# Spline coefficients inside the last context batch, ternary feed-forwards on seven tiles of 128 rows, a gate function and a scaling on ScalarE, spline units in another place

## The chip, the cores and the metric

The kernel runs on one core of a Trainium2 chip. The metric is device time in microseconds (us) of one execution; lower is better. Traces come from the hardware profiler on one such execution. TensorE multiplies, VectorE and ScalarE compute and drain PSUM, GpSimd (POOL) does small work, SyncE (SP) issues most transfers. TensorE's granted clock has two levels, 1.2 and 2.4 GHz; the profile writes them as 0.50 and 1.00.

## The reference

Four transformer layers, each an attention on x and a context and then a feed-forward, with a layer norm before and a residual after each of the eight parts. x is 8 batches of 112 rows of 512 numbers, the context 8 batches of 375 rows.

```
x = x + L0_xattn(ln(x), context)           # part 0, att0
x = x + L0_ffn(ln(x))                      # part 1, ffn0: ternary weights, sigmoid gate
x = x + L1_xattn(ln(x), context)           # part 2, att1: 16 heads, grouped
x = x + L1_ffn(ln(x))                      # part 3, ffn1: ternary weights, silu gate, Hadamard
x = x + L2_xattn(ln(x), context)           # part 4, att2: linear attention
x = x + L2_ffn(ln(x))                      # part 5: one ternary layer
x = x + L3_xattn(ln(x), context)           # part 6, att3
x = x + L3_ffn(ln(x))                      # part 7, ffn3: weights from spline control points

# L0_ffn; quant rounds each row to 8 bits by its own largest magnitude
h = sigmoid(quant(x) @ ternary(w_gate).T) * (quant(x) @ ternary(w_up).T)     # 2048 wide
y = quant(h) @ ternary(w_down).T
# L1_ffn
h = silu(quant(x) @ ternary(w_gate).T) * (quant(x) @ ternary(w_up).T)
y = quant(fwht(h)) @ ternary(w_down).T     # fwht: Walsh-Hadamard transform over the 2048
# L3_ffn: each dense weight is a cubic interpolation of control points
w[n] = cubic in the distance to the control point below, from four points around it
```

## The kernel before

Every engine runs one program written out by hand; they meet at semaphores. An engine executes in order, so what stands behind a waiting instruction waits too. A `Ring` hands PSUM banks round: names in their order of use, each with a lag in iterations; `wait_free`, `wait_filled` and `wait_drained` wait for a bank's last user, for TensorE's result, and for its reader. `link` makes a VectorE instruction wait for the one before it. SP issues transfers in the order of its own program, and waits in it.

**Context** (to 594 us). `context_part` goes over 8 batches; in each TensorE makes three thirds (k1, v1, k2, v2, v3 and transposes T), then k3, the last T and kv_0, kv_1. VectorE has about 4 us of work in each third and drains kv at the end. In batches 0 to 5 a ternary weight is made behind that; in batch 6 two of three spline matrices (L501 to L505) and `powers_of_q` (L520 to L539); in batch 7 the third matrix and `coefficients`, which works out the polynomials (L552 to L561) and splits them in three bf16 parts (L571, L574). ScalarE then repeats two of the parts (L443, L444), and only after that does TensorE transpose them. SP ends the stage with the stores of batch 7, the last of them behind kv_1's drain.

**Weights** (to 617). `weights_part`: SP loads wq3, wp3 and w2 behind `context["filled"]`, then x and the context of two batches of att0, then issues for each of 16 coefficient groups two stores. TensorE transposes a group; ScalarE copies it to one of 8 buffers (L670), and for groups 8 to 15 first waits until the stores of that buffer have landed. After group 3 it waits for the raw weights (L674). At its end ScalarE and TensorE turn two quantized matrices, and att0 starts.

**ffn0 and ffn1** (826 to 951, 1571 to 1814) are both `ternary_ffn`, over 8 tiles, one per batch, of 112 rows. In an iteration b0 is the newest tile and b1, b2, b3 the ones before it (in ffn0 b3 is b2). VectorE's order is: `quantize_x` of b0 (normalize L233, maximum L1025, small numbers, round L1040 and L1043, the result is xi), statistics of the next; four pieces of b1, each 512 columns of gate times up (L1081 and a maximum L1085 in ffn0; L1074 and L1077 in ffn1); in ffn0 `quantize_h`, whose L1049 to L1053 are five small numbers, L1054 scales 2048 columns and adds a constant that rounds, L1057 takes the constant off and clips; in ffn1 the butterflies of b2 (L1098, L1099), the maximum L1101 and `quantize_h`; then y of b3 is added to x (L244). TensorE's order is: for each of four pieces gate and up products of b1 (g, u) and transposes (of clipped h in ffn0; of h of b2 in ffn1); in ffn1 the products with the Hadamard matrix (w) and the transposes of clipped h of b3; then the transposes of xi of b0 (xiT), then y of b3. The next gates wait for this xiT drained. The five names u0 to u3 and y share three banks, so u1 waits for the y before it to be added. ScalarE does for each gate a tanh (L995), in ffn1 behind a copy of the gate (L994), and drains the transposes. x stays in `X`, batch by batch.

The last feed-forward, ffn3, already works on 7 tiles of 128 rows: SP copies pieces of `X` into tiles (L2136); a tile of 128 rows takes rows of two batches.

**att2** (1812 to 1985): `attention2` works on 8 batches in 11 iterations, and eight spline units are put in each iteration on TensorE, ScalarE and VectorE, numbered 8i to 8i+7. A unit makes part of ffn3's weights: one or four small products, a ScalarE copy, a VectorE predicated copy (L1579). Units share two banks, so TensorE's unit u waits for the copy of unit u-2:

```
spline["pe"](pe, 8 * i + 3)
if b2 is not None:            # products a0, a1
...
spline["pe"](pe, 8 * i + 4)
```

## Time and profile before

| | |
|---|---|
| median of three runs | 2653.1 us (2650.66 to 2653.58) |
| the profiled execution | 2655.79 us, span 2654.0 us, mean granted clock 0.952 |
| TensorE busy | 2320.2 us, 87% of the span |
| VectorE busy | 1250.8 us, 47% |
| ScalarE busy | 776.7 us, 29% |
| chain that ended last | TensorE 72%, VectorE 18%, ScalarE 5% |

The busy shares are means over stages with different limits. The chain is followed back from the last instruction, at each step to what released it. In a row, L12 is line 12 of the kernel, PE TensorE, DVE VectorE, ACT ScalarE, SPq SyncE's queue; "<-" names what ended the idle time. Ends of products are modelled; products that follow one another start closer together than their mean duration.

### The profile page before, as it was taken

The numbers are of one execution on the slowest core, as the hardware profiler recorded it, in microseconds if no ns is written. First come the engines' busy times: TensorE is split into PE (matmuls) and PEld (weight loads), VectorE is DVE, ScalarE is ACT, GpSimd is POOL, SyncE is SP. The second block draws the span as 40 slices with busy tenths as digits, with TensorE's granted clock in tenths as the row PEclk, the third lists the DMA queues.
The fourth block names the chain that finished last, engine by engine and source line by source line (L and its number), as shares of the span: only waits on it lengthen the run. The fifth ranks groups of instructions, "written<-read, shape, count | busy, mean of one in ns | idle before, by whom it ended". The sixth has DMA issues, their size and how long they took to land.

```text
span 2654.0 us, 27949 instructions
## 1 busy us (share of the span) xinstructions
PE 2320.2 (87%) x10524; PEld 1358.8 (51%) x10524; DVE 1250.8 (47%) x2497; ACT 776.7 (29%) x1611; POOL 148.7 (6%) x303
## 2 busy tenths in 40 slices
PE   8999999948887869999999986666877788889999
PEld 3555555536554536666666654443433455534444
DVE  1333333562115945555555558974444566621111
ACT  1322333113011323333333324432332455411111
POOL 0000000000000001110001000000000000000000
PEclk9999999979998989999999998887998899989999
DMA  5454433155113010300000030001000211100000
GB/s 200 157 214 159 154 149 122 67 172 211 47 58 159 1 29 19 120 18 24 20 23 24 15 96 17 1 1 31 14 12 7 71 47 47 48 4 4 8 4 12
DMA packets 48042, 171.68 MB, mean 65 GB/s; under 512 B 4561, under 2 KB 24337, under 8 KB 42110
## 3 DMA queue, kind: packets, MB, share of 16 engines
q1 hardware_dynamic: 46182, 132.14, 14.2%
q0 software_dynamic: 1728, 37.75, 3.7%
q8 instruction: 86, 1.41, 0.2%
q14 instruction: 46, 0.38, 0.0%
HBM read 121.58 MB, written 46.47 MB: 63 GB/s over the span
## 4 chain that ended last, share of the span: by engine, by line
PE 72%; DVE 18%; ACT 5%; issue 3%; DMA 1%; SPq 0%; POOL 0%; DVEq 0%; ACTq 0%; POOLq 0%
PE psum L118 61%; PE psum L111 6%; PE psum L1262 4%; DVE R L1098 1%; DVE small L2058 1%; DVE R L1099 1%; ACT WK L2008 1%; DVE small L1101 1%; DVE WK L233 1%; PE psum L1976 1%; DVE WK L1081 1%; DVE small L1085 1%; DVE R L1579 1%; DVE small L1430 1%; ACT R L670 1%
## 5 line engine op out<-in xcount | busy, mean ns | idle before, releaser
L118 PE MATMUL psum<-R,WK 128*125 128x512 f32 (+6 forms) x4000 | 1451.7, 513 | 106.1 <-DVE X L244 40.9
L118 PEld LDWEIGHTS psum<-R,WK 128*112 128x112 f32 (+3 forms) x4000 | 662.6, 176 | 758.1 <-issue 552.6
L111 PE MATMUL psum<-small,WK 112*125 112x112 f32 (+5 forms) x2252 | 309.8, 267 | 132.2 <-DVE WK L233 34.4
L111 PEld LDWEIGHTS psum<-small,WK 112*125 112x125 f32 (+5 forms) x2252 | 249.8, 154 | 241.6 <-issue 130.4
L118 PE MATMUL psum<-WK,R 128*128 128x112 f32 (+4 forms) x1152 | 260.4, 375 | 14.0 <-DVE R L1579 9.0
L118 PEld LDWEIGHTS psum<-WK,R 128*128 128x128 f32 (+2 forms) x1152 | 162.1, 183 | 85.0 <-issue 18.9
L118 PE MATMUL psum<-WK 125*112 125x128 f32 (+5 forms) x1280 | 198.2, 298 | 1.5 <-DVE WK L847 1.2
L118 PEld LDWEIGHTS psum<-WK 125*112 125x112 f32 (+2 forms) x1280 | 162.7, 177 | 66.6 <-issue 49.8
L1430 DVE TENSOR_REDUCE small<-psum 112x1 f32<-112x487 f32 x128 | 85.0, 664 | 221.4 <-PE psum L118 219.5
L1352 ACT ACTIVATE WK<-psum,small 112x487 f32<-112x487 f32 x128 | 96.9, 757 | 259.5 <-DVE small L1432 258.7
L1262 PE MATMUL psum<-R,WK 128*112 128x512 f32 x256 | 120.4, 593 | 0.6 <-ACT WK L1332 0.6
L2008 ACT ACTIVATE WK<-psum,small 112x375 f32<-112x375 f32 x128 | 72.2, 568 | 112.0 <-DVE small L2059 112.0
L2217 DVE SCALAR_TENSOR_TENSOR WK<-WK 128x512 f32<-128x512 f32 x28 | 19.4, 692 | 159.6 <-PE psum L111 141.9
L118 PE MATMUL psum<-R 125*128 125x128 f32 (+2 forms) x320 | 59.9, 298 | 35.4 <-DVE R L1579 33.9
L2058 DVE TENSOR_REDUCE small<-psum 112x2 f32<-112x750 f32 x64 | 59.8, 935 | 61.6 <-PE psum L118 61.3
L223 POOL TENSOR_SCALAR small<-small 112x1 f32<-112x1 f32 (+1 forms) x63 | 14.2, 225 | 1324.1 <-DVE small L217 1324.1
L1438 DVE COPY WK<-psum 125x336 f32<-125x336 f32 x128 | 64.3, 503 | 3.0 <-PE psum L111 3.0
L2187 ACT COPY WK<-psum 128x512 f32<-128x512 f32 x28 | 16.4, 585 | 164.5 <-PE psum L118 164.5
L118 PEld LDWEIGHTS psum<-R 125*128 125x128 f32 (+1 forms) x320 | 34.4, 155 | 56.4 <-DVE R L1579 45.4
L1567 ACT COPY R<-psum 128x256 f32<-128x256 f32 x96 | 35.2, 374 | 87.4 <-PE psum L118 87.2
L464 DVE TENSOR_TENSOR WK<-WK,small 125x512 f32<-125x512 f32 x24 | 16.6, 692 | 92.3 <-PE psum L111 75.3
L820 ACT COPY WK<-psum 128x448 f32<-128x448 f32 x32 | 17.0, 530 | 145.8 <-PE psum L118 76.5
(208 smaller groups left out, 2088.4 us busy)
## 6 DMA issues: line engine op xcount, KB each, us to landing
R<-in_wf POOLq DMA_DIRECT2D x6, 4096.0 KB, 13.7
d_w<-R POOLq DMA_DIRECT2D x6, 2048.0 KB, 17.9
R<-d_w SPq DMA_DIRECT2D x6, 2048.0 KB, 13.0
WK<-in_ctxT SPq DMA_DIRECT2D x16, 750.0 KB, 5.8
d_v<-WK SPq DMA_DIRECT2D x16, 750.0 KB
R<-in_wq SPq DMA_DIRECT2D x7, 1024.0 KB, 6.9
R<-in_wo SPq DMA_DIRECT2D x6, 1024.0 KB, 16.2
d_k<-X SPq DMA_DIRECT2D x8, 750.0 KB, 3.2
```

The source lines that it names most:

```text
L111: ins = pe.transpose(dst, src, idn[0:k, 0:k])
L118: ins = pe.matmul(dst, lhs, rhs, start=k == 0, stop=k == len(pairs) - 1)
L233: return dve.tensor_scalar(dst, x, mv[0:rows, k % 2, 0:1], rv[0:rows, k % 2, 1:2], ALU.subtract, ALU.mult)
L670: act.copy(coefT[0:84, k % 8].rearrange("p s q -> p (s q)"), bank[k % 4][0:84, :].bitcast(BF16)).then_inc(sem("coefT_ready"), 1)
L1081: dve.scalar_tensor_tensor(piece, th[:, c % 2, :], 1.0, dve_ring.bank[f"u{c}"][0:T, :], ALU.add, ALU.mult).then_inc(dve_ring.sem_drained, 1)
L1262: ins = pe.matmul(y, oT[:, g % 2, h, :], wo[:, 4 * g + h, :], start=4 * g + h == 0, stop=4 * g + h == NH - 1)
L1352: act.activation(prob[:, k % 3, :], act_ring.bank[f"s{j}"][0:T, 0:SK], ACT.Exp, bias=nmax[:, k % 3:k % 3 + 1], scale=rq[:, (NG * b + g) % ...
L1430: link(dve.tensor_reduce(mx[:, k:k + 1], act_ring.bank[f"s{j}"][0:T, 0:SK], AX, ALU.max, negate=True))
L1438: dve.tensor_copy(probT[0:SP, j % 2, 0:NS, :], src[0:SP, 0:NS * T].rearrange("p (i t) -> p i t", i=NS))
L1567: ins = act.copy(home(k, t), pieces_of(u)[0])
L2008: act.activation(prob[:, k, a, :], s_ring.bank[f"s{h}"][0:T, 0:S], ACT.Exp, bias=nmax[:, k, a:a + 1], scale=scale, accum_out=total[b % 2][ ...
L2058: link(dve.tensor_reduce(mx[:, j % 2, :], both[:, :, 0:S], AX, ALU.max, negate=True))
```

## The change

The spline coefficients are taken apart: `coefficients(dve, link, w)` does one matrix, `split_coefficients` the split. Batch 6 makes all three spline matrices; the powers, the coefficients and the split lie between the thirds of batch 7. The loads of the raw weights wait for `raw_free`, which is two results of the last third, in place of the context's last results. Ring semaphores are shared by stages.

Both ternary feed-forwards work on 7 tiles of 128 rows. SP copies pieces of `X` into seven tiles xf (`sync`) and, tile by tile after its add, back (`back`); the attention behind each of them waits for all of these copies on every engine (`x_ready` with n of 2 or 4). In ffn1 the gate is one `Silu` on ScalarE, without the copy and without L1074. The scaling of L1054 is done by ScalarE (`scale`, 2048 columns, `Identity` with a scale and a bias per row); VectorE gives it its number (`scale_of_h`) and clips afterwards (`quantize_h`). On VectorE `quantize_x` stands behind the pieces, in ffn0 behind `scale_of_h` and ahead of the clip; in ffn1 the clip of b3 stands between the pieces and `quantize_x`. TensorE's order in these stages is as before.

In att2 unit 8i+4 stands ahead of a0 and a1 on TensorE and VectorE, and unit 8i+6 ahead of the add on VectorE.

```diff
+            if n in (2, 4):
+                eng.wait_ge(sem(f"{'ffn0' if n == 2 else 'ffn1'}_back"), 16 * sum(len(list(pieces(i))) for i in range(NT)))
+            elif n:
...
+                        if b == NB - 1:
+                            if s == 0:
+                                powers_of_q(dve, link)
+                                coefficients(dve, link, 0)
+                            if s == 1:
+                                coefficients(dve, link, 1)
+                                coefficients(dve, link, 2)
+                            if s == 2:
+                                split_coefficients(dve, link)
...
+                    elif b == 6:
+                        dve.wait_ge(sem("spline_inputs"), 16 * 5)
+                        for w in range(3):
...
+            def raw_free(eng):
+
+                act_ring.wait_filled(eng, NB - 1, f"v2_{NS - 1}")
+                dve_ring.wait_filled(eng, NB - 1, f"k2_{NS - 1}")
...
-                context["filled"](sp)
+                context["raw_free"](sp)
...
+            def sync(sp):
+
+                if hadamard:
+                    last_values(sp)
+                for i in range(NT):
+                    if i >= 2:
+                        sp.wait_ge(sem(f"{stage}_x{i % 2}"), arrived[i - 2])
+                    for b, of, to in pieces(i):
+                        updates[n - 1].wait_drained(sp, b, "y")
+                        sp.dma_start(xf[i][to, :], xr[of, b, :]).then_inc(sem(f"{stage}_x{i % 2}"), 16)
+
+            def back(sp):
+
+                for i in range(NT):
+                    dve_ring.wait_drained(sp, i, "y")
+                    for b, of, to in pieces(i):
+                        sp.dma_start(xr[of, b, :], xf[i][to, :]).then_inc(sem(f"{stage}_back"), 16)
+
...
+                def scale(b, src):
+                    act.wait_ge(sem(f"{stage}_down"), b + 1)
+                    if b:
+                        act.wait_ge(sem(f"{stage}_hi"), b)
+                    act.activation(scaled, src, ACT.Identity, bias=magic, scale=rs).then_inc(sem(f"{stage}_scaled"), 1)
+
+                for bs in iterations(3 + H, NT):
...
-                            src = act_ring.bank[f"g{c}"][0:T, :]
-                            if silu:
-                                act.copy(gc[:, c % 2, :], src)
-                            act.activation(th[:, c % 2, :], src, ACT.Tanh, scale=half[:, b1 % 2:b1 % 2 + 1]
-                                           ).then_inc(act_ring.sem_drained, 1)
+                            src = act_ring.bank[f"g{c}"][:, :]
+                            act.activation(th[:, c % 2, :], src, ACT.Silu if silu else ACT.Tanh,
...
+                    if not hadamard and b1 is not None:
+                        scale(b1, h)
...
+                    if hadamard and b2 is not None:
+                        scale(b2, w0)
...
-                def quantize_h(b, src):
+                def scale_of_h(b):
                     s = b % 2
                     dve.wait_ge(sem(f"{stage}_scales"), b + 1)
                     link(dve.tensor_scalar(hm, hm, ch[:, b % 3:b % 3 + 1], 1e-5, ALU.mult, ALU.max))
                     link(dve.tensor_scalar(hm, hm, 1.0 / qb, None, ALU.mult))
                     link(dve.reciprocal(rh, hm))
-                    link(dve.tensor_scalar(rh, rh, ch[:, b % 3:b % 3 + 1], None, ALU.mult))
-                    link(dve.tensor_scalar(ysc[:, s:s + 1], hm, ws[0:T, m0 + 2:m0 + 3], None, ALU.mult))
-                    link(dve.tensor_scalar(src, src, rh, MAGIC, ALU.mult, ALU.add))
+                    if b:
+                        dve.wait_ge(sem(f"{stage}_scaled"), b)
+                    dve.tensor_scalar(rs, rh, ch[:, b % 3:b % 3 + 1], None, ALU.mult).then_inc(sem(f"{stage}_down"), 1)
+                    dve.tensor_scalar(ysc[:, s:s + 1], hm, ws[:, m0 + 2:m0 + 3], None, ALU.mult
+                                      ).then_inc(sem(f"{stage}_ysc"), 1)
+
+                def quantize_h(b):
+                    dve.wait_ge(sem(f"{stage}_scaled"), b + 1)
                     if b:
                         act_ring.wait_filled(dve, b - 1, f"hi{FC - 1}")
-                    dve.tensor_scalar(hi, src, -MAGIC, 127.0, ALU.add, ALU.min).then_inc(sem(f"{stage}_hi"), 1)
...
+                for bs in iterations(3 + H, NT):
                     b0, b1, b2, b3 = bs[0], bs[1], bs[2], bs[2 + H]
-                    if b0 is not None:
-                        quantize_x(b0)
-                        if b0 + 1 < NB:
-                            ln_stats(dve, link, n, b0 + 1)
                     if b1 is not None:
                         if b1 and not hadamard:
-                            dve.wait_ge(sem(f"{stage}_hi"), b1)
+                            dve.wait_ge(sem(f"{stage}_scaled"), b1)
                         for c in range(FC):
                             piece = h[:, c * 512:(c + 1) * 512]
                             act_ring.wait_drained(dve, b1, f"g{c}")
+                            if hadamard and b2 is not None:
+                                act_ring.wait_filled(dve, b2, f"h{c}")
+                            dve_ring.wait_filled(dve, b1, f"u{c}")
                             if silu:
-                                if hadamard and b2 is not None:
-                                    act_ring.wait_filled(dve, b2, f"h{c}")
-                                link(dve.scalar_tensor_tensor(piece, th[:, c % 2, :], 1.0, gc[:, c % 2, :],
-                                                              ALU.add, ALU.mult))
-                                dve_ring.wait_filled(dve, b1, f"u{c}")
-                                dve.tensor_tensor(piece, dve_ring.bank[f"u{c}"][0:T, :], piece, ALU.mult
+                                dve.tensor_tensor(piece, dve_ring.bank[f"u{c}"][:, :], th[:, c % 2, :], ALU.mult
                                                   ).then_inc(dve_ring.sem_drained, 1)
                             else:
-                                dve_ring.wait_filled(dve, b1, f"u{c}")
-                                dve.scalar_tensor_tensor(piece, th[:, c % 2, :], 1.0, dve_ring.bank[f"u{c}"][0:T, :],
+                                dve.scalar_tensor_tensor(piece, th[:, c % 2, :], 1.0, dve_ring.bank[f"u{c}"][:, :],
                                                          ALU.add, ALU.mult).then_inc(dve_ring.sem_drained, 1)
-                            dve_ring.wait_drained(dve, b1, f"u{c}")
-                            if not hadamard:
+                                dve_ring.wait_drained(dve, b1, f"u{c}")
                                 link(dve.tensor_reduce(hmax[:, c:c + 1], piece, AX, ALU.max,
                                                        apply_absolute_value=True))
                         if not hadamard:
                             link(dve.tensor_reduce(hm, hmax, AX, ALU.max))
-                            quantize_h(b1, h)
+                            scale_of_h(b1)
+                    if hadamard and b3 is not None:
+                        quantize_h(b3)
+                    if b0 is not None:
+                        quantize_x(b0)
+                        if b0 + 1 < NT:
+                            stats(b0 + 1)
+                    if not hadamard and b1 is not None:
+                        quantize_h(b1)
...
-                        quantize_h(b2, src)
+                        scale_of_h(b2)
                     if b3 is not None:
-                        add_to_x(dve, dve_ring, b3, ysc[:, b3 % 2:b3 % 2 + 1])
+                        dve.wait_ge(sem(f"{stage}_ysc"), b3 + 1)
+                        add_to_x(dve, dve_ring, b3, ysc[:, b3 % 2:b3 % 2 + 1], xf[b3])
...
                     spline["pe"](pe, 8 * i + 3)
+                    spline["pe"](pe, 8 * i + 4)
                     if b2 is not None:
...
-                    spline["pe"](pe, 8 * i + 4)
...
+                    spline["dve"](dve, 8 * i + 4)
...
-                    spline["dve"](dve, 8 * i + 4)
                     spline["dve"](dve, 8 * i + 5)
+                    spline["dve"](dve, 8 * i + 6)
                     if b3 is not None:
                         add_to_x(dve, dve_ring, b3)
-                    spline["dve"](dve, 8 * i + 6)
...
-                  ternary_ffn("ffn1", 3, 3, 128.0, True, True), attention2("att2", 4), ternary_layer("layer", 5),
+                  ternary_ffn("ffn1", 3, 3, 128.0, True, True, lambda sp: stages[2]["last_values"](sp)), attention2("att2", 4), ternary_layer("layer", 5),
...
-            stages[2]["load"](sp)
+            stages[2]["load"](sp, stages[1]["sync"])
+            stages[1]["back"](sp)
             if upto > 2:
                 stages[2]["sync"](sp, stages[3]["load"])
             if upto > 3:
+                stages[3]["sync"](sp)
                 x_ready(sp, 3)
                 spline["load_early"](sp)
                 for n in (4, 5, 6):
                     stages[n]["load"](sp)
+            if upto > 3:
+                stages[3]["back"](sp)
             for n in range(4, min(upto, 7)):
                 if n == 4:
                     x_ready(sp, n)
```

## Rows read from the trace of the kernel before

**Rows 1.** Busy us of each engine by window, then clock, DMA share, GB/s.
```profile
826.00:951.00 125.00, 101.43 (x547) 59.08 (x545) 106.59 (x217) 41.28 (x72) 5.91 (x16) 0.95 0.21 85
...
1570.00:1812.00 242.00, 156.18 (x925) 108.48 (x924) 199.99 (x288) 88.89 (x168) 8.09 (x16) 0.82 0.10 31
...
1812.00:1985.00 173.00, 134.84 (x506) 64.94 (x505) 74.33 (x196) 54.36 (x127) 5.91 (x16) 0.93 0.08 20
...
592.00:596.00 4.00, 1.69 (x16) 1.72 (x17) 3.79 (x11) 2.77 (x2) 0.00 (x0) 0.50 0.16 59
...
846.00:849.00 3.00, 0.35 (x2) 0.00 (x0) 2.89 (x5) 0.21 (x1) 0.00 (x0) 1.00 1.02 423
...
849.00:852.00 3.00, 2.89 (x11) 1.63 (x12) 2.79 (x10) 1.18 (x2) 0.00 (x0) 0.54 1.01 421
```

**Rows 2.** Timeline of the end of the context: start us, us, engine, line.
```profile
491.02 2.15 DVE L501 TENSOR_TENSOR R<-R 128x1920 f32<-128x1920 f32 x1
...
507.49 7.01 DVE L539 SCALAR_TENSOR_TENSOR R<-R 128x128 bf16<-128x128 bf16 x24
...
559.28 2.15 DVE L501 TENSOR_TENSOR R<-R 128x1920 f32<-128x1920 f32 x1
...
575.65 0.97 SPq L753 DMA_DIRECT2D WK<-in_ctx  x1
...
594.31 6.47 PE L111 MATMUL psum<-small,R 128*84 128x128 bf16 x64 [35.74 <-ACT R L444]
...
600.92 11.05 ACT L670 COPY R<-psum 84x1024 bf16<-84x1024 bf16 x12
```

**Rows 3.** DMA issues from 559 to 568: KB each, us from issue to landing.
```profile
X<-in_x SPq DMA_DIRECT2D x8, 224.0 KB, 10.7
...
R<-in_w SPq DMA_DIRECT2D x1, 1024.0 KB, 10.8
```

**Rows 4.** ffn0, the instructions of L1043: ns least/median/most, first and last start.
```profile
L1043 DVE TENSOR_SCALAR WK<-WK x8: 426/427/428, 832.3 to 921.4; 112x512 bf16<-112x512 f32 x8
```

**Rows 5.** Timeline of ffn0 in its steady part.
```profile
884.96 0.69 DVE L1081 SCALAR_TENSOR_TENSOR WK<-WK,psum 112x512 f32<-112x512 f32 x1
...
887.73 1.29 DVE L1054 TENSOR_SCALAR WK<-WK,small 112x2048 f32<-112x2048 f32 x1
...
890.86 0.54 DVE L233 TENSOR_SCALAR WK<-X,small 112x512 f32<-112x512 f32 x1
...
893.42 0.43 DVE L1043 TENSOR_SCALAR WK<-WK 112x512 bf16<-112x512 f32 x1
...
898.00 5.39 PE L118 MATMUL psum<-R,WK 128*112 128x512 bf16 x24 [1.20 <-ACT WK L981]
```

**Rows 6.** Groups of ScalarE over the whole span: busy us, mean ns, idle before.
```profile
L438 ACT ACTIVATE R<-R 128x2048 bf16<-128x2048 f32 x24 | 45.5, 1904 | 0.0
...
L398 ACT ACT_TABLE_LOAD x1 | 1.3, 1283 | 0.7 <-PEq L2355 0.7
```

**Rows 7.** ffn1, the instructions of L1101.
```profile
L1101 DVE TENSOR_REDUCE small<-R x8: 2286/2286/2287, 1611.5 to 1799.1; 112x1 f32<-112x2048 f32 x8
```

**Rows 8.** Timeline of ffn1.
```profile
1659.05 1.23 DVE L1098 TENSOR_TENSOR R<-R 112x1024 f32<-112x1024 f32 x1 [2.45 <-ACT R L1010]
...
1672.09 1.29 DVE L1054 TENSOR_SCALAR R<-R,small 112x2048 f32<-112x2048 f32 x1
...
1675.35 1.96 PE L118 MATMUL psum<-R,WK 128*112 128x512 bf16 x4 [7.98 <-DVE X L244]
```

**Rows 9.** Copies of L2136 from X into a tile, before the last feed-forward.
```profile
DMA to landing us min/median/max: 2.0/2.5/8.8
```

**Rows 10.** att2, waits: us in total, times, longest.
```profile
PE psum L118 <- DVE R L1579: 35.8, 30, 7.9
```

**Rows 11.** Timeline of att2.
```profile
1888.67 0.39 PE L118 MATMUL psum<-R 84*128 84x512 bf16 x1 [1.96 <-DVE R L1579]
...
1893.63 0.40 PE L118 MATMUL psum<-R 84*128 84x128 bf16 x4 [0.92 <-DVE R L1579]
```

174 lines of the change are left out of this document (92 added, 82 removed).

## The prediction

> **What bounds the kernel now.** I read the busy time of each engine by stage first [rows 1]. In the first feed-forward, ffn0, VectorE is busy for 106.59 of 125 us and TensorE for 101.43. In the second, ffn1, VectorE has 199.99 of 242 us at a granted clock of 0.82, so TensorE idles enough to lose its clock. In att2 TensorE is busy for 134.84 of 173 us: it is the bound, with gaps. What stands at the end of the context stage can't be read from shares, so I took the timeline [rows 2]: after batch 7 VectorE does spline work alone from 559.28, and TensorE's next transposes start at 594.31 after 35.74 us idle, released by ScalarE's repeat copies, which take 6.2 of it: VectorE's part ends at 588.1. The profiled execution took 2655.79 us (span 2654.0, 1.8 around it); the median of the runs shown is 2653.1, 2.7 below, so I sum against 2655.8 and take off 2.7.
>
> **Context: the wait goes, another stands behind it.** Batch 6 takes the third matrix (5.9 us: from 491.02 to 502.8 it does two) and loses the powers (11.7 us, ending at 507.49 + 7.01 = 514.5). Batch 7 then takes powers and one matrix after v3_0 (11.7 + 3.2), two matrices after v3_1 (7), the split after v3_2 (what the 28.8 us from 559.28 to 588.1 leave after a matrix of 5.9 and coefficients of some 10.4: 12.5). A third of a batch gives VectorE some 17.6 us and asks 4 of it, so each insert ends inside; the last starts some 14.5 us before 559.28 and so ends near 557.3, and kv_0 and kv_1 are drained about 0.4 us later than now. The split is then ready near 557.3 instead of 588.1, and TensorE could start near 563.5: 31 us earlier. I don't count that. SP issues the raw weights behind the last store, which waits for kv_1, so the new condition raw_free frees nothing: they are issued from 559.8 as now, and w2 lands 10.8 us after its issue at 560.7 [rows 3], at 571.5. ScalarE waits for it after four of its sixteen coefficient copies. Four more follow at 0.92 us each (twelve take 11.05 [rows 2]) until about 577. The ninth overwrites the first buffer and waits until its stores have landed; SP issues those behind x and four context loads, the last at 575.65 [rows 2]. The DMA share is still 0.16 at 592 to 596 [rows 1], that is, a few of the sixteen engines finish the last load near 595, and I take each to work in order. So copies nine to sixteen run from 596.5 to 603.9, not from about 604.5 to 611.9: **-8 us**. If the stores pass the loads, the copies end at 571.5 + 2.1 + 11 = 584.6: -27. If the eight pairs of stores drain more slowly than the copies ask, -5.
>
> **ffn0: fewer tiles, but a longer loop.** Now it has eight starts of L1043 (xi) from 832.3 to 921.4 [rows 4], 14.0 us apart once the loop is full: VectorE computes quantize_x at the head of an iteration while TensorE does gates and ups, and is never idle. The edit takes L1054 (1.29 us) off VectorE, which as a share of busy time would give 12.6 us a tile. But it also puts quantize_x behind the pieces, and TensorE's order is unchanged: gates and ups of b1, xiT of b0, then y. It now waits for xi with y queued behind, and the next gates need that same xiT. One loop, from xi to xi:
> - xiT, y and 32 gate and up products: 48 products at 0.217 us (24 of them take 5.39 [rows 5]) are 10.4, the transposes and the crossings to ScalarE and VectorE 1.5: 11.9.
> - last piece, its reduction, hm and the small ones: 884.96 to 887.73, 2.8 [rows 5].
> - quantize_x: 890.86 to 893.42 plus 0.43, 3.0; less 0.5 because two small ones leave the way and the engine overlaps neighbours: together 5.2 for both.
>
> That is 17.0 at full clock. TensorE idles some 5.5 us in each loop. After a shorter idle stretch (0.35 of 3 us busy at 846 to 849) the granted clock was 0.54 over the next 3 us, so nearly all of them at the lower level of 1.2 GHz [rows 1]; in ffn1, after 7.98 us idle, four products took 1.96 us [rows 8]. Three us at half pace lose 1.6 to 1.8: 18.8 a loop. Seven tiles: 15.1 and 15.8 for the first two, which have no y or only a start-up, and 4 x 18.8 make 106.1 us from the first xi to the last, against 89.1 now. The tail from the last xi is 12 + 1.6 to u3, 2.8, the ScalarE scaling 2.1, clip 1.2, transposes and drains 2.6, y and add 4.2, and 1.4 for the clock: 27.9, against 29.3 now (921.8 to the last add's end at 951.1). So 134.0 against 118.4: **+15.5**; +5 if the clock stays up, +18 if it stays low longer. The scaling of 2048 columns is not in this trace: a 2048-column ScalarE pass took 1904 ns [rows 6], two operands read per row cost some 0.1 each, 2.1. It is hidden behind quantize_x except in the tail.
>
> **ffn1.** Each tile's butterflies end in a maximum, L1101; by its first and last start they are 26.8 apart with a short last one of 17.7, so 28.3 before it [rows 7]. The edit removes a VectorE pass (L1074, as long as L1081's 0.69) in each of four pieces, L1054 of 1.29 [rows 8], and one small operation: 4.3 us a tile. It does not all come back, since ScalarE scales behind the last VectorE number and its queue holds the next gate behind that, and since u1 needs the bank of y, freed by the add (7.98 us of waiting for L244 at 1675.35 now [rows 8]). The loop: butterflies, maximum and small ones 12.5 (1659.05 to 1672.09 less one small and a link); last small one and add 0.8; u1 to the last piece 7.5, which is today's course of TensorE after the add, from 1675.35, at low clock first; piece and clip 1.75; quantize_x and statistics 3.9. Together 26.5. The stage: 34 to the first butterfly (31 now; quantize_x comes later), five loops of 26.2 (the late ones have no quantize_x), one of 22, a tail of 24, and 3.5 by which such a sum falls short of today's 242: 214.5, **-28**. If the clock stayed high, -36; if the gates wait longer on ScalarE, -22.
>
> **Copies in and back.** Tiles 0 to 5 arrive while the attention before still runs; tile 6 arrives one transfer after its end, long before its use. At both stages' ends all engines now wait for the last tile back in X: two issues and a landing. The same kind of copy from X took 2.0/2.5/8.8 us (least, median, most) [rows 9]; with 0.4 us per issue and 2.7 for the 224 KB piece, 3.2 each: **+6.4** (5 to 8). SP's other loads lie in front of these in its queue, but are through by then.
>
> **Silu.** The trace has one table load, 1283 ns at the start [rows 6]; Tanh and Exp share it. Silu may need another before ffn1 and the old one after it, both in front of the first work of a stage: **+2.6**, or 0. The Trainium skill (ScalarE: Activation LUTs, "What ACT_TABLE_LOAD costs" and "Table sets") puts every switch of set at about 2.66 us with its drain, estimated 5.3 for two, against the load alone here; and it says that copy and identity are in every set, so by it no switch would come inside ffn1. No run so far shows either.
>
> **att2.** Unit 8i+6 on TensorE waits for unit 8i+4's copy on VectorE, now behind the whole of o: 1.96 us idle at 1888.67. The unit two after 8i+6 waits behind add_to_x: 0.92 at 1893.63 [rows 11]. In all 35.8 us in 30 waits [rows 10]. Both copies move ahead of those operations. What it costs: unit 8i+4 now stands ahead of a0 and a1, must wait for unit 8i+2's copy (0.9), and puts 1.1 us of products later on o's chain. Net 1.7 us in each of five full iterations, less in the others: **-9** (-12 to -3).
>
> **Sum.** -8 + 15.5 - 28 + 6.4 + 2.6 - 9 = -20.5. 2655.8 - 20.5 = 2635.3 profiled, 2632.6 as a median: 2633.
>
> **The rivals.**
> - Stores pass the loads: context gives 27, not 8: 2614. For it: TensorE and VectorE are free. Against: x, issued behind 3 MB of weights, lands only with them (10.7 us for 224 KB) [rows 3]. 0.15.
> - ffn0 follows VectorE's busy time: 12.6 x 7 against 14.0 x 8, with 3 of ends: -12 instead of +15.5: 2605. Against: the order of waits above. 0.10.
> - The serial loops cost more: ffn0 +18, ffn1 -22, context -5, att2 -3, copies +7, tables +2.6: -2.4, 2650. 0.10.
> - Slower: ScalarE needs a table load at each change between Silu and the copies of ffn1, eight a tile. They lie in the 7.5 us stretch where TensorE and VectorE wait for the gates: 8 x 1.28 = 10 a tile, 72 in seven tiles: 2633 + 69 = 2702. It decides from 3 us a tile, two or three loads. Nothing in this trace has Silu beside a copy; Tanh beside copies needs none. 0.04.
>
> The forecast as worked out has 0.61, with a range of 2618 to 2645 of its own. Over all cases I give 2608 to 2648. A measurement here can tell about 0.2% (5 us): faster than 2647.8 has 0.89, within 0.06, slower 0.05.
>
> **What would show it.** TensorE's first coefficient transposes at 563 to 565 and a ScalarE wait for a DMA of some 19 us before the ninth copy; ffn0's L1043 successor every 18 to 19 us with TensorE idle 5 to 6 us before xiT, in a stage of about 140 us; ffn1's butterflies every 26 to 27 us; 3 us between the last add and the next stage; one or two table loads; att2 near 164 us. The prediction is wrong if ffn0 gets shorter, if the ninth copy doesn't wait, or if table loads repeat.

## The result, and the profile after

The kernel after takes 2633.9 us (median of 4 runs, 2631.5 to 2636.9) against 2652.9 of the kernel before (4 runs, 2650.7 to 2653.6): a ratio of 0.993, 95% interval 0.9913 to 0.9948, so 0.7% faster. Forecast were 2633.0 and a range of 2608 to 2648. The profiled execution took 2632.73 us (span 2630.8) against 2655.79 (2654.0): 23.1 less, where the ledger said 20.5.

I cut both traces at the end of the last add of each stage, which starts a window below and ends the one before it. Busy time by window of the kernel after, for ffn0, ffn1 and att2, the answer to [rows 1]:

```profile
816.90:958.30 141.40, 96.73 (x476) 45.14 (x476) 83.43 (x182) 54.08 (x70) 9.67 (x14) 0.86 0.23 88
1581.70:1800.20 218.50, 144.02 (x812) 87.61 (x812) 144.62 (x211) 82.81 (x127) 12.19 (x14) 0.81 0.14 43
1800.20:1965.90 165.70, 135.13 (x502) 65.28 (x502) 75.03 (x198) 55.17 (x129) 5.91 (x16) 0.91 0.09 23
```

In a row stand the window, its length, the busy time of TensorE's products, its weight loads, VectorE, ScalarE and GpSimd with their numbers of instructions, then the granted clock, the DMA share and GB/s. VectorE's share falls in both ternary stages (from 85% to 59% in ffn0), and ffn0 still gets longer. The ledger by stage, us:

| stage | before | after | change | forecast |
|---|---|---|---|---|
| to att0's first transposes | 617.3 | 609.2 | -8.0 | -8 |
| att0, to its last add | 210.5 | 207.7 | -2.9 | 0 |
| ffn0 | 123.3 | 141.4 | +18.1 | +15.5 |
| att1 | 620.3 | 623.4 | +3.1 | +3.2 |
| ffn1 | 242.7 | 218.5 | -24.2 | -28 + 1.3 |
| att2 | 172.3 | 165.7 | -6.6 | -9 + 3.2 + 1.3 |
| the rest | 667.5 | 664.9 | -2.6 | 0 |
| sum | 2654.0 | 2630.8 | -23.1 | -20.5 |

Each column is one trace, and a stage's time varies from trace to trace. In the traces of the experiments below that leave a stage as it is, ffn0 took 142.3 to 145.2 us (six traces), ffn1 216.6 to 218.5, att0 206.0 to 210.6, and att0's first transposes came at 608.9 to 613.0. The kernel after's 141.4 for ffn0 is the least of all seven, so ffn0's change is +18 to +22 rather than +18.1.

The end of the context, timeline of the kernel after, against [rows 2]:

```profile
563.36 5.53 PE L111 MATMUL psum<-small,R 128*84 128x128 bf16 x64 [4.94 <-ACT R L452]
...
571.65 1.91 ACT L697 ACTIVATE R<-R 128x2048 f32<-128x2048 f32 x1 [3.46 <-DMA R<-in_w]
...
596.03 7.40 ACT L693 COPY R<-psum 84x1024 bf16<-84x1024 bf16 x8 [18.76 <-DMA d_cd<-R]
```

TensorE starts 31 us earlier (563.36 against 594.31), and the ninth coefficient copy then waits 18.76 us for the stores of the first. Why the stores are late is in SyncE's queue:

```profile
567.95 8.19 SPq L773 DMA_DIRECT2D WK<-in_ctxT  x1
576.18 1.11 SPq L776 DMA_DIRECT2D WK<-in_ctx  x1
577.33 9.16 SPq L651 DMA_DIRECT2D d_cgu<-R  x1
586.53 0.59 SPq L651 DMA_DIRECT2D d_cd<-R  x1
```

The second number is the duration of the issue itself. Most issues here take 0.3 to 0.6 us; the third context load takes 8.19. The first store, whose data are ready since about 565, gets its turn at 577.33 and its issue takes 9.16, so that the second store of the pair (d_cd) is issued only at 586.53.

One tile of ffn0 in its steady part, against [rows 5]:

```profile
892.42 0.43 DVE L1102 TENSOR_SCALAR WK<-WK 128x512 bf16<-128x512 f32 x1
...
892.91 0.61 PE L111 MATMUL psum<-small,WK 128*128 128x128 bf16 x4 [5.50 <-DVE WK L1102]
...
893.31 7.51 PE L118 MATMUL psum<-R,WK 128*128 128x512 bf16 x24
...
907.53 0.69 DVE L1142 TENSOR_REDUCE small<-WK 128x1 f32<-128x512 f32 x1
...
909.33 2.09 ACT L1034 ACTIVATE WK<-WK,small 128x2048 f32<-128x2048 f32 x1 [1.81 <-DVE small L1113]
909.33 0.54 DVE L241 TENSOR_SCALAR WK<-R,small 128x512 f32<-128x512 f32 x1
...
911.90 0.43 DVE L1102 TENSOR_SCALAR WK<-WK 128x512 bf16<-128x512 f32 x1
```

From xi to xi it is 19.48 us. TensorE waits 5.50 us for xi; the 24 products behind it, y among them, then take 7.51 us where [rows 5] has 5.39; and VectorE takes 4.4 from the last reduction to the next xi. The seven starts of xi give the loop, the answer to [rows 4]; below them, who waited for this line:

```profile
L1102 DVE TENSOR_SCALAR WK<-WK x7: 427/427/428, 821.5 to 931.9; 128x512 bf16<-128x512 f32 x7
its engine sat idle before it (us, times) until:
who waited for it (us, times):
  PE psum L111: 39.4, 7
```

The butterflies' maximum in ffn1, against [rows 7], and the wait for the copy back at the start of att2:

```profile
L1168 DVE TENSOR_REDUCE small<-R x7: 2286/2286/2287, 1628.2 to 1783.4; 128x1 f32<-128x2048 f32 x7
```

```profile
1799.46 0.75 DVE L252 SCALAR_TENSOR_TENSOR R<-psum,small,R 128x512 f32<-128x512 f32 x1 [9.51 <-PE psum L118]
1803.46 0.69 DVE L224 BATCH_NORM_STATS2 small<-X 112x6 f32<-112x512 f32 x1 [3.25 <-DMA X<-R]
```

### The profile page after: what moved, and what is told of

Same layout as the page of the kernel before. It is cut to its first block, busy times and chain, and to the rows that moved or that the text cites. A ratio compares the mean times of both kernels' runs of the same rounds, so it can differ in the third digit from the quotient of the medians.

```text
span 2630.8 us, 27448 instructions
## 1 busy us (share of the span) xinstructions
PE 2301.4 (87%) x10340; PEld 1325.3 (50%) x10340; DVE 1173.3 (45%) x2385; ACT 784.4 (30%) x1569; POOL 156.5 (6%) x300
## 4 chain that ended last, share of the span: by engine, by line
PE 74%; DVE 15%; ACT 5%; issue 3%; SPq 2%; DMA 2%; POOL 0%; DVEq 0%; ACTq 0%; POOLq 0%
PE psum L118 63%; PE psum L111 7%; PE psum L1331 4%; DVE small L2127 1%; DVE R L1165 1%; ACT WK L2077 1%; DVE R L1166 1%; DVE WK L241 1%; PE psum L2045 1%; DVE small L1168 1%; SPq L651 1%; DVE small L1499 1%; DMA R<-in_wkv 0%; DVE R L1648 0%; DVE small L1085 0%
## 5 line engine op out<-in xcount | busy, mean ns | idle before, releaser
L118 PE MATMUL psum<-R,WK 128*125 128x512 f32 (+7 forms) x3872 | 1429.7, 520 | 82.9 <-DVE R L252 24.5
L118 PEld LDWEIGHTS psum<-R,WK 128*112 128x112 f32 (+4 forms) x3872 | 626.5, 172 | 752.7 <-issue 568.2
L111 PE MATMUL psum<-small,WK 112*125 112x112 f32 (+7 forms) x2196 | 310.3, 271 | 170.1 <-DVE WK L1102 50.8
L111 PEld LDWEIGHTS psum<-small,WK 112*125 112x125 f32 (+7 forms) x2196 | 249.0, 156 | 278.7 <-issue 138.3
L118 PEld LDWEIGHTS psum<-WK,R 128*128 128x128 f32 (+2 forms) x1152 | 161.1, 182 | 83.9 <-issue 17.4
L231 POOL TENSOR_SCALAR small<-small 112x1 f32<-112x1 f32 (+1 forms) x61 | 19.6, 322 | 1320.5 <-DVE small L225 1320.5
L1331 PEld LDWEIGHTS psum<-R,WK 128*112 128x112 f32 x256 | 40.1, 176 | 33.8 <-issue 33.0
## 6 DMA issues: line engine op xcount, KB each, us to landing
R<-in_wf POOLq DMA_DIRECT2D x6, 4096.0 KB, 13.7
```

Of the source, the lines that this page charges most:

```text
L111: ins = pe.transpose(dst, src, idn[0:k, 0:k])
L118: ins = pe.matmul(dst, lhs, rhs, start=k == 0, stop=k == len(pairs) - 1)
L1331: ins = pe.matmul(y, oT[:, g % 2, h, :], wo[:, 4 * g + h, :], start=4 * g + h == 0, stop=4 * g + h == NH - 1)
```

## The experiments

Each kernel is the kernel after with one edit, unless it says otherwise, and each was timed beside the kernel before. I compare them with the 2633.9 of the kernel after, through their ratios to before, and by stage; a stage's time is that of one trace, with the scatter given above.

**ffn0: quantize_x at the head again.**

```diff
                 for bs in iterations(3 + H, NT):
+                    if not hadamard and b0 is not None:
+                        quantize_x(b0)
+                        if b0 + 1 < NT:
+                            stats(b0 + 1)
                     if b1 is not None:
...
-                    if b0 is not None:
+                    if hadamard and b0 is not None:
                         quantize_x(b0)
```

> The kernel after, with quantize_x and the statistics of the next tile put back at the head of VectorE's iteration in ffn0 alone. Theory A (the serial loop: TensorE waits for xi with y queued behind it): xi is then made some 9 us before TensorE asks for it, TensorE's idle stretch of 5.5 us before xiT and the low clock behind it go, and the loop is VectorE's own chain: 11.9 us busy, 2.2 of waiting for ScalarE's scaling, some 0.7 of hand-overs, 14.8 against 19.0 to 20.0 now. Over five full loops that is -21 to -26: ffn0 about 117 us instead of 141.4, the kernel 2610 (2606 to 2616). Rival B (tiles of 128 rows and the scaling pass on ScalarE set the loop, wherever quantize_x stands): ffn0 stays above 136, the kernel within 5 us of 2634.

Measured: 2604.6 us, ratio 0.9825 (0.981 to 0.9839), just under the 2606 to 2616 of theory A. ffn0 takes 115.1 us instead of 141.4 to 145.2, which covers the gain of 29. The second xi now follows the first by 4.8 us, as in the kernel before, and the others are 14.5 to 15.2 us apart:

```profile
L1102 DVE TENSOR_SCALAR WK<-WK x7: 426/427/429, 823.1 to 901.3; 128x512 bf16<-128x512 f32 x7
its engine sat idle before it (us, times) until:
who waited for it (us, times):
  PE psum L111: 5.9, 1
```

Theory A holds and rival B falls: tiles of 128 rows with the scaling on ScalarE do a tile in 14.5 us in this order. What is left of waiting is VectorE's, for that scaling:

```profile
880.12 2.09 ACT L1034 ACTIVATE WK<-WK,small 128x2048 f32<-128x2048 f32 x1 [3.16 <-DVE small L1113]
...
882.24 1.23 DVE L1121 TENSOR_SCALAR WK<-WK 128x2048 bf16<-128x2048 f32 x1 [2.04 <-ACT WK L1034]
```

**ffn0: y ahead of xiT on TensorE.**

```diff
+                    if not hadamard and b3 is not None:
+                        act_ring.wait_drained(pe, b3, f"hi{FC - 1}")
+                        dve_ring.wait_free(pe, b3, "y")
+                        product(pe, dve_ring.bank["y"][:, :], [(hiT[:, ft, :], wd[:, ft, :]) for ft in range(FT)]
+                                ).then_inc(dve_ring.sem_filled, 1)
                     if b0 is not None:
                         pe.wait_ge(sem(f"{stage}_xi"), b0 + 1)
...
-                    if b3 is not None:
+                    if not (not hadamard) and b3 is not None:
```

> The kernel after, with TensorE issuing y of the oldest tile before xiT of the newest in ffn0 alone; VectorE's order stays as in the kernel after. Theory A: y (about 3.5 to 7.5 us at whichever clock, with 0.7 of waiting for the last copy) then runs while VectorE does the small numbers and quantize_x, and leaves the loop; 19.5 becomes about 15.5, the kernel 2614 (2609 to 2620). If what is serial is not y but the way from the last piece to xi and back to the first gate, little comes: 2630. Rival B: no change, 2634 within 5.

Measured: 2613.1 us, ratio 0.9855 (0.984 to 0.987). ffn0 takes 126.1 us. Its first two intervals are 17.3 and 17.4 us, the others 14.5 and 16.2 in turn. In these TensorE waits for the next xi only 1.19 us, with y behind it no more:

```profile
880.65 3.63 PE L118 MATMUL psum<-R,WK 128*128 128x512 bf16 x16 [0.68 <-ACT WK L1033]
885.47 0.40 PE L111 MATMUL psum<-small,WK 128*128 128x128 bf16 x4 [1.19 <-DVE WK L1107]
```

So the loop has the two halves that the prediction gave it, and either cut frees it: y out of the queue behind the wait, or xi ahead of it.

**ffn1: quantize_x at the head.** The same edit as the first, for the other stage.

> The kernel after, with quantize_x and the statistics at the head of VectorE's iteration in ffn1 alone. Theory A: the loop from butterfly to butterfly loses part of the 3.9 us that quantize_x and the statistics take ahead of the butterflies, because at the head VectorE waits for the first gate anyway (u1 waits for the bank of y, which the add frees just before); six loops of 26.4 become about 24.9, and the first butterfly comes some 1 to 2 us earlier: -9, kernel 2625 (2620 to 2630). Rival: quantize_x now delays the first pieces by as much as it saves, because the first gate is ready earlier than I think: no change, 2634 within 5.

Measured: 2623.7 us, ratio 0.9894 (0.9877 to 0.9912). ffn1 takes 205.8 instead of 218.5 us; the butterflies are 24.4 to 26.2 apart instead of 26.0 to 27.1, and the first one comes 6.5 us earlier in its stage. That is more than the 9 expected: half of the gain lies ahead of the first butterfly, where 1 to 2 us were expected, and about 1 us of it, in the tail, is within the scatter.

**SyncE: context loads behind the first stores.**

```diff
-            def stores(sp):
+            def stores(sp, loads):
                 for k in range(16):
+                    if k == 8:
+                        loads(sp)
...
-            stages[0]["sync"](sp, range(2))
-            weights["stores"](sp)
+            weights["stores"](sp, lambda sp: stages[0]["sync"](sp, range(0, 2)))
```

> The kernel after, with SyncE issuing the four context loads of att0's first two batches behind the first eight pairs of coefficient stores instead of ahead of them. Theory C (the ninth coefficient copy waits for stores that stand behind 3 MB of loads, whose very issue takes 8 to 9 us each when the queue is full): stores are issued from about 567, land behind x at some 579, the ninth copy starts near 580 instead of 596.0 and the sixteenth ends near 588 instead of 603.4; then VectorE's int8 weights, which end near 594, set the rest: att0's first transposes near 598 instead of 609.2: -11, kernel 2623 (2618 to 2627). Rival D (the copies are held by w2 or by the DMA traffic itself): the ninth copy still waits until after 590, and att0 starts within 3 us of now, or later for its contexts: 2634 within 5.

Measured: 2620.7 us, ratio 0.988 (0.9861 to 0.9899). The ninth copy waits 1.35 us, and the store is issued in 0.43:

```profile
579.48 7.40 ACT L695 COPY R<-psum 84x1024 bf16<-84x1024 bf16 x8 [1.35 <-DMA d_cd<-R]
```

```profile
567.28 0.43 SPq L653 DMA_DIRECT2D d_cgu<-R  x1
...
579.92 2.18 SPq L775 DMA_DIRECT2D WK<-in_ctxT  x1
582.14 0.71 SPq L778 DMA_DIRECT2D WK<-in_ctx  x1
582.90 9.49 SPq L653 DMA_DIRECT2D d_cgu<-R  x1
```

Theory C holds in that the copies waited for stores queued behind the loads. The long issue has moved with the loads: it is now that of the first store of the ninth pair, 9.49 us, where no copy waits for it. What makes an issue long no run here shows; the "full queue" of the expectation stays a guess, and of the four loads in the kernel after only one took 8.19 us. att0's first transposes start at 593.8 instead of 609.2; its last add ends 12.5 earlier.

**att2: the spline units at their old places.**

```diff
-                    spline["pe"](pe, 8 * i + 4)
                     if b2 is not None:
...
+                    spline["pe"](pe, 8 * i + 4)
...
-                    spline["dve"](dve, 8 * i + 4)
                     if b2 is not None:
...
+                    spline["dve"](dve, 8 * i + 4)
                     spline["dve"](dve, 8 * i + 5)
-                    spline["dve"](dve, 8 * i + 6)
                     if b3 is not None:
                         add_to_x(dve, dve_ring, b3)
+                    spline["dve"](dve, 8 * i + 6)
```

> The kernel after, with the spline units of att2 at their old places on TensorE and VectorE (unit 8i+4 behind a0 and a1 and behind o, unit 8i+6 behind add_to_x). att2 went from 172.4 to 165.7 us, add to add, although its start now waits for the copy back (some 3 us) and for a table load (1.3). Theory A (the two releases that stood behind o and add_to_x): undoing it gives back 6.7 + 3.1 + 1.3 = 11: kernel 2645 (2642 to 2648). Rival (the stage got shorter because of a higher clock or fewer transfers beside it, not by the order): less than 4 us, 2634 to 2638.

Measured: 2645.6 us, ratio 0.9974 (0.9965 to 0.9982). att2 takes 174.8 instead of 165.7 us. TensorE's waits for L1648 from 1800 to 1985 us, in us, number and longest, of the kernel after and of this one, in that order, against [rows 10]:

```profile
PE psum L118 <- DVE R L1648: 27.7, 28, 6.7
```

```profile
PE psum L118 <- DVE R L1648: 37.6, 31, 6.9
```

From add to add, which ends att2 at 1965.9 and at 1981.0, they are 24.0 us in 25 waits and 34.7 in 30. Of these 10.7 us TensorE's other waits give back 1.4, and 9.1 show in the stage: the gain is that of the order. The clock is not the cause (0.91 after, 0.92 here).

**ffn1: Tanh in place of Silu.** `ACT.Silu if silu else ACT.Tanh` becomes `ACT.Tanh`; the gate of ffn1 is another function and its output another.

> The kernel after, with Tanh in place of Silu in the gate of ffn1: another function, so another output, but the same instruction count, shapes and operands; it measures the table loads alone. Theory A (two more loads of 1283 ns, each in front of work that others wait for): one load in the trace instead of three, kernel 2631.3. Theory B (they lie in idle time of ScalarE while TensorE does the first products): 2634. These differ by what one run scatters, so the trace decides: whether the first gate and the first Tanh of att2 come earlier by 1.3 us against the products that feed them.

Measured: 2631.6 us, ratio 0.9916 (0.9903 to 0.993), not to be told from the kernel after (0.9913 to 0.9948). The trace decides. The kernel after, before the first Silu and before the first Exp of att2 (L1753; the expectation calls it a Tanh):

```profile
1587.54 0.58 ACT L1028 COPY WK<-psum 128x512 bf16<-128x512 bf16 x1 [10.27 <-PE psum L111]
1588.14 1.28 ACT L1046 ACT_TABLE_LOAD   x1
1590.10 0.69 ACT L1046 ACTIVATE WK<-psum,small 128x512 f32<-128x512 f32 x1 [0.68 <-PE psum L118]
...
1817.95 1.28 ACT L1753 ACT_TABLE_LOAD   x1
1824.36 0.63 ACT L1753 ACTIVATE WK<-WK 112x512 f32<-112x512 f32 x1 [5.12 <-DVE WK L1783]
```

The Tanh variant, the same two places:

```profile
1592.78 0.58 ACT L1028 COPY WK<-psum 128x512 bf16<-128x512 bf16 x1 [10.27 <-PE psum L111]
1595.35 0.69 ACT L1046 ACTIVATE WK<-psum,small 128x512 f32<-128x512 f32 x1 [1.98 <-PE psum L118]
...
1826.89 0.63 ACT L1753 ACTIVATE WK<-WK 112x512 f32<-112x512 f32 x1 [5.59 <-DVE WK L1783]
```

The first gate starts 2.56 us after that copy with the load and 2.57 without it: the load fills time in which ScalarE waits for TensorE anyway, and at 1817.95 time in which it waits for VectorE. Theory B holds on the path. The stages of this trace are 1.9 and 2.0 us shorter (ffn1 216.6, att2 163.7), but not by the loads: the variant with att2's old order has both loads and the same 216.6 us in ffn1, and the variant with the gate of before, below, has neither and takes 165.5 us in att2.

**ffn1: the scaling on VectorE.**

```diff
-                    if hadamard and b2 is not None:
+                    if hadamard and not (hadamard) and b2 is not None:
                         scale(b2, w0)
...
                     dve.tensor_scalar(ysc[:, s:s + 1], hm, ws[:, m0 + 2:m0 + 3], None, ALU.mult
                                       ).then_inc(sem(f"{stage}_ysc"), 1)
+                    if hadamard:
+                        dve.wait_ge(sem(f"{stage}_down"), b + 1)
+                        if b:
+                            dve.wait_ge(sem(f"{stage}_hi"), b)
+                        dve.tensor_scalar(scaled, w0 if hadamard else h, rs, MAGIC, ALU.mult, ALU.add
+                                          ).then_inc(sem(f"{stage}_scaled"), 1)
```

> The kernel after, with the scaling of h in ffn1 as a VectorE pass of 1.3 us behind the small numbers, ahead of the add, and no ScalarE pass of 2.1 us. Theory A (the loop runs over VectorE from the first butterfly to the add and then over TensorE, whose u1 waits for the bank of y that the add frees; ScalarE's pass lies beside it): VectorE's part grows by 1.3 to 1.4 us in each of six tiles, and the end gains 0.8: +7, kernel 2641 (2638 to 2644). Rival B (the gates that queue behind ScalarE's 2.1 us pass hold the loop): taking it away saves up to 2.1 - 1.4 a tile, 0 to -5, kernel 2629 to 2634.

Measured: 2628.7 us, ratio 0.9911 (0.9897 to 0.9924); ffn1 takes 212.2 instead of 218.5 us. Its time can't be told from that of the kernel after (the intervals overlap), but the 2641 of theory A is excluded, and the stage shows what happened. The mechanism of theory A is there, and it is outweighed: the four full loops are 29.1, 28.1, 26.9 and 26.7 us against 27.0, 27.1, 26.4 and 26.3, 4 us more, but the first one is 23.0 instead of 26.0, the last 16.2 instead of 22.4 and the tail 0.9 shorter (within the scatter), 10 us less. The last tile shows why. TensorE in the kernel after, then ScalarE there, then ScalarE here:

```profile
1756.86 1.91 PE L111 MATMUL psum<-small,WK 128*128 128x128 f32 x16
1767.39 5.77 PE L118 MATMUL psum<-R,WK 128*128 128x128 f32 x32 [8.62 <-ACT WK L1050]
```

```profile
1764.19 2.09 ACT L1034 ACTIVATE R<-R,small 128x2048 f32<-128x2048 f32 x1 [10.86 <-DVE small L1113]
1766.19 2.02 ACT L1050 COPY WK<-psum 128x512 f32<-128x512 f32 x4
```

```profile
1763.47 2.05 ACT L1050 COPY WK<-psum 128x512 f32<-128x512 f32 x4 [4.16 <-PE psum L111]
1771.55 2.05 ACT L1061 COPY R<-psum 128x512 f32<-128x512 f32 x4 [6.03 <-DVE R L1120]
```

In the kernel after, the last tile is transposed by 1758.8, but its copies (L1050) queue behind the scaling of the tile before, which waits 10.86 us for VectorE, and TensorE idles 8.62 us for them. Here they are done while VectorE works, and the w copies (L1061) wait only for their buffer. I had looked at the full loops alone, where ScalarE is idle beside the pass.

**ffn1: the gate of before**, a copy, Tanh and two VectorE passes a piece, on seven tiles (the factors of Tanh change with it):

```diff
+                            if silu:
+                                act.copy(gc[:, c % 2, :], src)
-                            act.activation(th[:, c % 2, :], src, ACT.Silu if silu else ACT.Tanh,
+                            act.activation(th[:, c % 2, :], src, ACT.Tanh,
...
+                                link(dve.scalar_tensor_tensor(piece, th[:, c % 2, :], 1.0, gc[:, c % 2, :],
+                                                              ALU.add, ALU.mult))
-                                dve.tensor_tensor(piece, dve_ring.bank[f"u{c}"][:, :], th[:, c % 2, :], ALU.mult
+                                dve.tensor_tensor(piece, dve_ring.bank[f"u{c}"][:, :], piece, ALU.mult
```

> The kernel after, with the gate of ffn1 as it was before: a ScalarE copy and a Tanh per piece, and two VectorE passes of 0.69 us per piece, on seven tiles. Theory A (the pieces wait for TensorE at 2.2 us each, so the added passes show only behind the last piece of a tile; 28 us less came from one tile less): +0.75 us in seven tiles, less the 2.6 of two table loads that go: kernel 2637 (2634 to 2640). Rival B (ffn1 follows VectorE's busy time, so the shorter gate gave most of the gain): 28 passes of 0.69 are +19, less 2.6: kernel 2650.

Measured: 2639.2 us, ratio 0.9951 (0.9939 to 0.9964). VectorE's busy time in ffn1 rises from 144.62 to 164.96 us, the stage from 218.5 to 222.2 only:

```profile
1584.80:1807.00 222.20, 141.04 (x799) 87.66 (x812) 164.96 (x245) 94.75 (x154) 12.19 (x14) 0.82 0.14 42
```

Theory A holds and rival B's 2650 falls: the pieces wait for TensorE, and 20 us of VectorE's work are worth 3.7 (5.3 less 2.6 for table loads were expected, and the loads turned out to be free; with the scatter of ffn1 it is 3.7 to 5.6).

**Combinations.** The kernel after with quantize_x at the head in both stages and the context loads later:

> The kernel after, with quantize_x at the head in ffn0 and ffn1 and the context loads behind the first eight pairs of coefficient stores. The three parts lie in different stages and each was measured alone: 24.7, 11.9 (stage 218.5 to 205.8) and 12.5 less than the kernel after. If they add up: 2634 - 49 = 2585 (2580 to 2590). Rival: part of one is given back where the stages meet (a copy in or weights that are late for an earlier start): 2595 or more.

Measured: 2579.2 us, ratio 0.9728 (0.9715 to 0.9741), just under the 2580 to 2590 expected. The parts add up, nothing is given back. On this kernel two edits were tried in turn. The scaling pass behind the add, and not on ScalarE:

```diff
-                    if hadamard and b2 is not None:
-                        scale(b2, w0)
...
                         add_to_x(dve, dve_ring, b3, ysc[:, b3 % 2:b3 % 2 + 1], xf[b3])
+                    if hadamard and b2 is not None:
+                        dve.wait_ge(sem(f"{stage}_down"), b2 + 1)
+                        if b2:
+                            dve.wait_ge(sem(f"{stage}_hi"), b2)
+                        dve.tensor_scalar(scaled, w0, rs, MAGIC, ALU.mult, ALU.add
+                                          ).then_inc(sem(f"{stage}_scaled"), 1)
```

> The combined kernel (quantize_x first in both, loads later), and the scaling of ffn1 as a VectorE pass of 1.3 us behind add_to_x, not on ScalarE. With the pass ahead of the add, full loops were 1.1 longer (28.1 against 27.0) and the first, the last and the tail 3.0, 6.2 and 1 shorter. Theory A2 (the loss is the later add, for which TensorE's u1 waits; the gain is ScalarE's w copies and gates that no longer queue behind the pass): behind the add, the loops stay at the combined kernel's and the ends keep their gain: 8 us less than the combined kernel, 2577. Rival: VectorE's quantize_x and first pieces come 1.3 later and the loop with them: no less than the combined kernel, perhaps 4 more.

Measured: 2574.6 us, ratio 0.9709 (0.9696 to 0.9723); its interval touches that of the combined kernel. ffn1 201.5 instead of 205.4 us: the last interval is 16.9 instead of 23.4, but the other five changed by -1.0 to +1.8 and are 2.4 longer in all. That is half of what A2 expected. And y in the bank of u2:

```diff
-                                       range(5, 8), [(f"u{c}", 1) for c in range(FC)] + [("y", 2 + H)], tiles=NT)
+                                       (5, 6, 7, 5, 7), [(f"u{c}", 1) for c in range(FC)] + [("y", 2 + H)], tiles=NT)
```

> The combined kernel, with y in the PSUM bank of u2 instead of that of u1, in both ternary stages. Theory A (in ffn1 TensorE idles 4.96 us before u1 until the add has freed the bank, and runs u1, h1 and part of g2 at the low clock behind it): u1, h1 and g2 then run beside the butterflies, and what follows the add is shorter by the products of 8 matmuls and 4 transposes, 2.0 to 2.9 us in each of six tiles, less what ScalarE's gates (1.3 us each pair, behind its pass of 2.1) then hold: -8 in ffn1, 0 to -2 in ffn0: 2577. Rival: th has two buffers and the third gate waits for the first piece, which comes only after the add, so that ScalarE and VectorE set the time: within 3 us of the combined kernel.

Measured: 2573.9 us, ratio 0.9707 (0.9694 to 0.972). Its interval, too, touches that of the combined kernel. ffn1 takes 200.8 us, ffn0 115.2 (114.9 in the combined kernel); TensorE's wait for the add is 2.79 us instead of 4.95, and ScalarE's gate makes a new one of 0.97 behind it, between the two theories:

```profile
1656.51 1.04 PE L118 MATMUL psum<-R,WK 128*128 128x512 bf16 x4 [2.79 <-DVE R L252]
1658.52 1.08 PE L111 MATMUL psum<-small,WK 128*128 128x128 f32 x4 [0.97 <-ACT WK L1048]
```

All of it, with ffn0's scaling on VectorE too:

> The combined kernel with y in the bank of u2, ffn1's scaling on VectorE behind the add, and ffn0's scaling on VectorE ahead of quantize_h. ffn0: VectorE waits 2.04 us a tile for ScalarE's pass of 2.09 and would do it in 1.3 itself: 0.7 less in each of seven tiles, -5. ffn1: the last interval between butterflies was 6.5 shorter with the pass behind the add (16.9 against 23.4), the loops 1.2 to 1.9 shorter with the bank of u2: if both hold, -5 against the kernel with the bank alone. Together 2573.9 - 10 = 2564 (2560 to 2569). Rival: with the bank free early, VectorE's 1.3 us behind the add delays the first piece and with it the gates (th has two buffers): ffn1 gains nothing more, 2569 to 2574.

Measured: 2563.3 us (2560.6 to 2565.6), ratio 0.9667 (0.9654 to 0.968): 3.3% below the kernel before and 2.7% below the kernel after. ffn0 takes 106.8 us, its loop 13.7; ffn1 takes 197.9.

## Why the prediction was right

**Context, -8 forecast, -8.0 measured.** TensorE started at 563.36 (forecast near 563.5), the ninth copy at 596.03 after 18.76 us (596.5, some 19). The wait is the stores', as the experiment with the loads moved shows. One part of the reasoning was half of what happens: I took the stores to be issued from 576 on and to wait in the DMA engines' queues. Half of the 18.76 us is SyncE's, held at the issue of the first store until 586.5; the other 9.5 us, to 596.03, lie between the issue of the second store and its landing. The two together gave the time that was forecast for the one, which is luck.

**ffn0, +15.5 forecast, +18.1 measured.** The serial loop is shown from both sides, by moving xi and by moving y. In the tile above, xi to the end of u3 took 14.25 us (892.42 to 906.67), where I had 11.9 and 1.8 for the clock; u3 to the next xi 5.23, where I had 5.2. The term that was mis-sized is mostly the clock's: 24 products took 7.51 us against 5.39, 2.1 more where 1.6 to 1.8 was forecast, and the four full intervals were 18.5 to 20.0 (77.9 in all, against 4 x 18.8 = 75.2). The first two made 1.6 more than forecast, the tail (26.4 against 27.9) 1.5 less. These are of the trace with the shortest ffn0; in five of the six others the first two intervals were 16.9 to 17.5 us each against the 15.1 and 15.8 forecast, the tail was 28.8, and the granted clock of the stage was 0.82 or 0.83 instead of 0.86. So the forecast for the stage is short by 3 to 6 us.

**ffn1, -28 forecast, -24.2 measured.** The full loops came nearly as worked out (26.0 to 27.1 against 26.2 to 26.5, the last 22.4 against 22; 2.2 more in all). The ends did not: 36.9 us to the first butterfly instead of 34, 26.4 from the last one instead of 24. The 3.5 us that the forecast added without naming a wait for them covered most of it. Ahead of the first butterfly quantize_x comes late: with quantize_x at the head the first butterfly came 30.4 us into its stage. I had priced the move mainly for the loop. Where the gain comes from is shown by parts: the gate gives 3.7 us; against it the late quantize_x costs 12.7 and the scaling on ScalarE, as placed, 6.3, each with some 2 us of scatter and measured alone. That leaves some 39 us of gain, the larger part, for the one tile less and the clip moved behind the pieces, which were not tried apart.

**Copies, +6.4 forecast.** 3.25 us of waiting for the copy back into X at att2's start, and att1 3.1 longer: right in size and place.

**Silu, +2.6 forecast, 0 found on the path.** Both loads are in the trace at the places named, and both lie in idle time. The step that failed is "both in front of the first work of a stage": the first work of ScalarE there is a copy, and the first Silu has products to wait for. The Trainium skill (ScalarE: Activation LUTs, "What ACT_TABLE_LOAD costs") puts a switch at about 2.66 us with its drain. The trace shows 1283 ns for each load; from the end of the copy before it to the start of the first gate are 1.98 us, load included, and the gate started no later than without it. By the Trainium skill (ScalarE: Activation LUTs, "Table sets") no load would come between Silu and copies. This trace agrees, with three loads in all.

**att2, -9 forecast, -9.1 measured** by undoing it; with the copy back, 172.3 + 3.25 - 9.1 is 166.5 against 165.7.

**What was not forecast:** 2.9 us less in att0 and 2.6 in the last stages. att0 took 206.0 to 210.6 us in the variants that do not touch it, and the single ternary layer 66.1 to 67.7 (67.5 before), so these are scatter. Behind the layer all thirteen traces with the change took 598.1 to 598.8 us, the one of the kernel before 600.0; why, no experiment shows. These and the Silu term cover the 6.4 us by which ffn0 and ffn1 came out longer. That the sum is right to 2.6 us is in part luck.

The rivals: that the stores pass the loads, that ffn0 follows VectorE's busy time, and that table loads repeat are all excluded by rows above. The price of the second was worked out wrong: 12.6 x 7 against 14.0 x 8 and 3 of ends is -21, not -12, and would have given about 2597. Of the rival with dearer serial loops one part came, ffn0 at +18.

## What to carry over

An engine's order decides before its busy time does: look at what stands behind each wait in the same queue, here y behind xi, the copies of the last tile behind a scaling pass, the stores behind loads. The change took 78 us of VectorE's busy time out of ffn0 and ffn1, and the two stages together got only 6 us shorter; three moves within the queues, with no work removed, gained 55 us. Price an edit at the first and the last tile as well as in the full loop: in ffn1, scaling on ScalarE saved 4 us in the loops and cost 10 at the first interval and the end.

## What the runs showed of the hardware

- A SyncE issue of a 750 KB load took 8.19 us, and that of a 105 KB store behind it 9.16, against 0.35 and 0.39 for other issues of the same instructions in the same trace. SyncE issues nothing else meanwhile. The runs don't show what makes an issue long. In the kernel with the loads moved the long issue (9.49 us) came again at the first store behind four such loads.
- A table load of 1283 ns started 0.02 us behind the end of the instruction before it (at 1588.14 and 1817.95), not when the data for the next function arrived: both times it ran while ScalarE had nothing to do.
- After idle stretches of 5.5 us in each 19.5 us, TensorE's granted clock was 0.86 over ffn0 (0.82 to 0.86 in the other traces with that order), so a part of the products at the lower of 1.2 and 2.4 GHz; with the wait gone it was 0.93 over the stage.
